# Splitting one PSUM eviction between ScalarE and VectorE, and taking a statistics sum ahead of the first product, in a fused normalise, shift and convolve kernel

## The chip, the cores and the metric

One Trainium2 chip, one core. The metric is the time of one execution on the device in microseconds (us). The measured times are medians of several executions; a profile is one execution taken by the hardware profiler.

## What is computed

The input x is 32 x 384 x 64 x 64 in f32 (batch, channel, row, column). Each group of 12 channels of an image is normalised over its 12 x 64 x 64 values. The normalised tensor is then moved, eight channels at a time, by one of 48 rounded offsets (pixels that come from outside are zero) and convolved with a 5x5 Gaussian whose centre carries the fraction of the offset. The input is added to the result:

```
x = x + _L0_conv_ref(_gn(x), L0_conv_offset)
disp = _displace(x.reshape(B, P, cpp, h, w), off_int).reshape(B, C, h, w)
sub = offset - lax.stop_gradient(off_round)
kernel = jnp.exp(-jnp.sum(d * d, axis=-1) / (2.0 * SIGMA ** 2))
out = lax.conv_general_dilated(disp, kw, ..., feature_group_count=C, ...)
```

Shift and Gaussian are separable, so that each is a product with a matrix along the rows and then one along the columns.

## The kernel before, in words

**Tiling.** A step handles 2 images x 24 channels (a superblock of channels). There are 16 superblocks and 16 steps in each: 256 steps, numbered t. The 24 channels lie as 4 lanes (32 partitions each) of 6 channels in 3 positions. A step's input fills one of 16 slots of `xin`; its result is added into the same slot, stored from there, and then the slot is loaded anew.

**Stages of a step.**
- VectorE takes statistics of each slot six steps ahead, in three pieces (`statistics`, line 440).
- GpSimd prepares `summands` (256, 258). For each pair of steps TensorE sums them over the partitions with a product against `ones` (`sum_stats`, 600), VectorE reduces that (`sums`, 447), and GpSimd makes scale and bias (`coefficients`, 273 to 284), two pairs ahead.
- ScalarE normalises one half of the slot (546) and GpSimd the other (293) into `norm`.
- TensorE forms the row product into `yp` (`y_product`, 608). `yp` has four PSUM banks, one for each lane, and one buffer only.
- ScalarE evicts all of `yp` to `y` in one instruction of 1536 columns (`copy_y`, 555). It signals `y_ready`.
- TensorE forms the column product into `xp` (`x_product`, 617), position 2 first, then 0 and 1.
- VectorE adds `xp` to the slot in two instructions: `add_x` part 0 (459, 512 columns), part 1 (462, 1024 columns). ScalarE issues the stores (571), SyncE the loads (194).

**Order on TensorE.** `two_steps` (639) covers a pair. With Y(t) for the row products of a step, X(t) for its column products and S for `sum_stats`, the order in the steady state is Y(t), X(t-1), S, Y(t+1), X(t), Y(t+2), X(t+1), S, and so on. So X always lies between two Y, and hides the eviction; between X(t-1) and Y(t+1) there is also an S, between X(t) and Y(t+2) there is none. I call a step with an S an even step and the one without an odd step. Waits ahead of a Y: `y_ready` (the eviction), `norm0_ready`, `norm1_ready`, `mats_ready`. S waits for `result0_ready`, that is for `add_x` part 0, since both use one PSUM bank.

**Order on VectorE.** A step (485) is: statistics 0 and 1 of the slot six ahead; in step 15 of a superblock `swap_rows` (424, three copies of new row matrices); `add_x` part 0 of t-1; statistics 2; `add_x` part 1; in step 0 `swap_columns` (430); in even steps `sums`; in step 9 `values` (414).

**Head.** Before the first product only the sum of pair 0 is taken. `sum_stats` for pair 1 comes after Y of the second step (662 to 664), and GpSimd's `coefficients(1)` (311) runs inside its step 0, after the normalisation of the second step. ScalarE's `normalise` of the third step needs those coefficients, and it stands ahead of `copy_y` of the second step in ScalarE's program.

All of this is an order written out by hand for each engine. The first and last superblocks are unrolled; the middle is a hardware loop.

Of the kernel before, what the change touches and what calls it, by code (L numbers as in the profile page):

```python
# [45 lines left out]
def displaced_conv(nc: bass.Bass, x: bass.AP, offset: bass.AP, out: bass.AP):  # L46
# [7 lines left out]
    with ExitStack() as ctx:  # L54
# [90 lines left out]
        norm1_free = sem("norm1_free")  # L145
        y_done = sem("y_done")
        y_ready = sem("y_ready")
        x_started = sem("x_started")
        x_done = sem("x_done")
        result0_ready = sem("result0_ready")  # L150
# [55 lines left out]
        def _(pool):  # L206
# [95 lines left out]
            normalise(0, 0, 0, first=True)  # L302
            column_matrices(0)
            make_summands(1, 1, early=True)

            def step(c, s, head, tail):
                t, p = STEPS * c + s, STEPS // PAIR * c + s // PAIR
                if not (tail and s == STEPS - 1):
                    normalise(t + 1, (s + 1) % STEPS, STEPS // PAIR * c + (s + 1) // PAIR, first=head and s == 0)
                if head and s == 0:  # L310
                    coefficients(1, 1, early=True, used=False)
                if not (tail and s // PAIR + LEAD >= STEPS // PAIR):
                    if s % PAIR == 0:
                        make_summands(p + LEAD, (s // PAIR + LEAD) % RING)
                    else:
                        coefficients(p + LEAD, (s // PAIR + LEAD) % 2)
                if not tail:
                    if s == 2:
                        whole_distances(c + 1)
                    if s == 4:  # L320
                        full_distances(c + 1)
                    if s == 10:
                        column_matrices(c + 1)
# [3 lines left out]
        def _(dve):  # L327
# [127 lines left out]
            def add_x(t, s, part):  # L455
# [4 lines left out]
                else:  # L460
                    at = xin[:, s, 0:4, :].rearrange("p (k h) f -> p h k f", h=QP)
                    nc.vector.tensor_tensor(at, xp[:, 0:2], at, ALU.add).then_inc(result1_ready, 1)  # L462

            def all_statistics(s):
                for part in range(CHUNKS):
                    statistics(0, s, part)
# [8 lines left out]
            all_gains()  # L475
            values(0)
            all_statistics(2)
            swap_columns(0)
            swap_rows(0)
            all_statistics(3)  # L480
            sums(1, 1, early=True)
            all_statistics(4)
            all_statistics(5)
# [1 line left out]
            def step(c, s, head, tail):  # L485
                t, p = STEPS * c + s, STEPS // PAIR * c + s // PAIR
                start = head and s == 0
                far = (s + AHEAD) % STEPS
                c_far = c + (s + AHEAD) // STEPS
                more = not (tail and s + AHEAD >= STEPS)  # L490
                s_old = (s - 1) % SLOTS
                ring_used = far % PAIR == 0 and not (head and s + AHEAD < PAIR * RING)
                if more:
                    statistics(c_far, far, 0, p + LEAD + 1 if ring_used else None)
                    statistics(c_far, far, 1)
                if s == STEPS - 1 and not tail:
                    swap_rows(c + 1)
                if not start:
                    add_x(t - 1, s_old, 0)
                if more:  # L500
                    statistics(c_far, far, 2)
                if not start:
                    add_x(t - 1, s_old, 1)
                if s == 0 and not head:
                    swap_columns(c)
                if s % PAIR == 0 and not (tail and s // PAIR + LEAD >= STEPS // PAIR):
                    sums(p + LEAD, (s // PAIR + LEAD) % 2, read=True)
                if not tail and s == 9:
                    values(c + 1)
# [5 lines left out]
        def _(act):  # L515
# [35 lines left out]
            def copy_y(t, v, first):  # L551
                act.wait_ge(y_done, t + 1)
                if not first:
                    act.wait_ge(x_done, ADDS * (t - 1))  # L554
                nc.scalar.activation(y[:, v].rearrange("p k r a m -> p a (k r) m"),  # L555
                                     yp[:, :, 0:POS * P].rearrange("p a (n m) -> p a n m", m=32),
                                     ACT.Copy).then_inc(y_ready, 1)

            square(0, 0)
# [35 lines left out]
        @block.tensor  # L595
        def _(pe):


            def sum_stats():
                nc.tensor.matmul(xp[:, 3, 1, 0:PAIR * GROUPS * 9], ones[:, :],  # L600
                                 summands[:].rearrange("p t n s -> p (t n s)"),
                                 start=True, stop=True).then_inc(stat_summed, 1)

            def y_product(k, v):
                for r in range(R):
                    for a in range(LANES):
                        rows = slice(32 * a, 32 * a + 32)
                        last = nc.tensor.matmul(yp[:, a, P * k:P * (k + 1)], norm[rows, v, r, P * k:P * (k + 1)],  # L608
                                                ay[rows, k, r, :], start=(r == 0), stop=(r == R - 1))
                if k == POS - 1:  # L610
                    last.then_inc(y_done, 1)

            def x_product(k, v):
                for r in range(R):
                    for h, m in ((0, 0), (1, 0), (0, 1), (1, 1)):
                        rows, outs = slice(64 * h, 64 * h + 64), slice(64 * m, 64 * m + 64)
                        last = nc.tensor.matmul(xp[outs, 2 * (k // 2) + h, k % 2, HW * r:HW * (r + 1)],  # L617
                                                y[rows, v, k, r].rearrange("p a m -> p (a m)")[:, outs], ax[rows, k],
                                                start=True, stop=True)
                if k > 0:  # L620
                    last.then_inc(x_done, 1)

            def x_products(v, results):

                pe.sem_inc(x_started, 1)
                x_product(2, v)
                pe.wait_ge(result1_ready, results)
                pe.sem_inc(x_started, 1)
                x_product(0, v)
                x_product(1, v)  # L630

            def begin_y(number, evicted):
                if evicted is not None:
                    pe.wait_ge(y_ready, evicted)
                pe.wait_ge(norm0_ready, number)
                pe.wait_ge(mats_ready[0], number)
                y_product(0, 0)

            def two_steps(one, head=False, more=True, last=False):

                two, three = one + 1, one + 2
                if not isinstance(one, int):
                    two, three = pe.snap(two), pe.snap(three)
                pe.wait_ge(norm1_ready, one)
                pe.wait_ge(mats_ready[1], one)
                y_product(1, 0)
                pe.wait_ge(mats_ready[2], one)
                y_product(2, 0)
                if not head:
                    pe.wait_ge(result0_ready, one)  # L650
                    x_products(1, one)
                    if more:
                        pe.wait_ge(summands_ready, one)
                        pe.wait_ge(result0_ready, two)
                        sum_stats()
                pe.wait_ge(y_ready, one)
                pe.wait_ge(norm0_ready, two)
                y_product(0, 1)
                pe.wait_ge(norm1_ready, two)
                y_product(1, 1)  # L660
                y_product(2, 1)
                if head:
                    pe.wait_ge(first_summands, LEAD)
                    sum_stats()
                    pe.wait_ge(first_sums, LEAD)
                    pe.wait_ge(summands_ready, one)
                    sum_stats()
                if more:
                    pe.wait_ge(sums_ready, one)
                pe.wait_ge(ax_ready, one)  # L670
                pe.wait_ge(result0_ready, two)
                x_products(0, two)
                if not last:
                    begin_y(three, two)

            pe.wait_ge(filled, FILLS)
            pe.wait_ge(first_summands, 1)
            sum_stats()
            begin_y(1, None)
            two_steps(1, head=True)  # L680
            with pe.Fori(PAIR + 1, PAIR * (PAIRS - LEAD) + 1, PAIR) as one:
                two_steps(one)
            for p in range(PAIRS - LEAD, PAIRS):
                two_steps(PAIR * p + 1, more=False, last=p == PAIRS - 1)
            pe.wait_ge(y_ready, TOTAL)
            pe.wait_ge(result0_ready, TOTAL + 1)
            x_products(1, TOTAL + 1)

# [20 lines left out]
```

## Time and profile before

| | |
|---|---|
| median of 3 runs | 1280.02 us (1278.77 to 1281.33) |
| profiled execution, its own time | 1280.09 us |
| its span, first to last instruction | 1278.3 us |
| mean granted TensorE clock | 0.994 |
| busy: TensorE matmul, VectorE, ScalarE, GpSimd | 94%, 77%, 55%, 51% |
| DMA | 403.06 MB, mean 315 GB/s |

Times in rows are us from the start of the span, durations in us or, where marked, ns. "PE" is TensorE's matmuls and "PEld" its weight loads, "DVE" VectorE, "ACT" ScalarE, "POOL" GpSimd. A name with q is the engine's queue. Profiled execution and median differ by 0.07 us.

### The profile page before, as it was taken

How to read it: one execution, taken by the hardware profiler on the slowest of the kernel's cores; microseconds unless marked ns; L12 is line 12 of the kernel's file. 1: busy time of each engine (PE TensorE's matmuls, PEld its weight loads, DVE VectorE, ACT ScalarE, POOL GpSimd, SP SyncE). 2: the span in 40 equal slices, each digit the busy share in tenths (PEclk: the TensorE clock that was granted, in tenths of full speed). 3: DMA queues.
4: the chain of work that ended last, by engine and by line, in shares of the span. 5: the costliest groups of instructions: out<-in, count | busy, mean ns of one | idle time of the engine just before them, and what ended most of it. 6: DMA issues, size and time to landing. Idle time of an engine off the chain costs nothing.

```text
span 1278.3 us, 110940 instructions
## 1 busy us (share of the span) xinstructions
PE 1200.4 (94%) x49408; PEld 1140.1 (89%) x49408; DVE 990.3 (77%) x1530; ACT 708.4 (55%) x595; POOL 658.1 (51%) x1478
## 2 busy tenths in 40 slices
PE   2899999999999999999999999999999999999995
PEld 2799999999999999999999999999999999999995
DVE  5788787778778778787778778778787788778862
ACT  3464655656555565655646555565555656555552
POOL 4645545554554645545554554645545554554540
PEclk9899999999999999999999999999999999999998
DMA  9699999999999999999999999999999999999854
GB/s 314 218 327 332 320 333 329 331 326 325 323 334 329 324 329 331 327 323 335 319 332 331 324 317 340 330 324 331 319 336 317 335 325 324 332 328 326 290 169 151
DMA packets 409768, 403.06 MB, mean 315 GB/s; under 512 B 16528, under 2 KB 409744, under 8 KB 409744
## 3 DMA queue, kind: packets, MB, share of 16 engines
q1 hardware_dynamic: 204944, 201.41, 48.9%
q10 hardware_dynamic: 204800, 201.36, 47.3%
q8 instruction: 12, 0.20, 0.1%
q14 instruction: 12, 0.10, 0.0%
HBM read 201.38 MB, written 201.33 MB: 315 GB/s over the span
## 4 chain that ended last, share of the span: by engine, by line
PE 81%; ACT 13%; issue 4%; DVE 1%; POOL 1%; ACTq 0%; POOLq 0%; DVEq 0%
PE yp L608 59%; PE xp L617 18%; ACT y L555 13%; PE xp L600 3%; DVE stats L440 0%; ACTq L554 0%; DVE xin L462 0%; POOL t_int L231 0%; POOL t_full L237 0%; POOL grid_i L211 0%; POOL var L280 0%; POOL rstd L282 0%; POOL norm L293 0%; DVE both L447 0%; DVE sub L378 0%
## 5 line engine op out<-in xcount | busy, mean ns | idle before, releaser
L608 PE MATMUL yp<-ay,norm 32*128 32x128 f32 x24576 | 762.3, 275 | 45.2 <-ACT y L555 35.3
L608 PEld LDWEIGHTS yp<-ay,norm 32*128 32x128 f32 x24576 | 716.9, 188 | 65.1 <-issue 50.7
L555 ACT ACTIVATE y<-yp 128x1536 f32<-128x1536 f32 x256 | 371.5, 1451 | 467.5 <-PE yp L608 467.5
L440 DVE BATCH_NORM_STATS2 stats<-xin 128x6 f32<-128x512 f32 x768 | 509.4, 692 | 0.1
L617 PE MATMUL xp<-ax,y 64*64 64x64 f32 x24576 | 420.8, 221 | 5.9 <-issue 4.6
L617 PEld LDWEIGHTS xp<-ax,y 64*64 64x64 f32 x24576 | 384.7, 135 | 37.4 <-issue 6.9
L459 DVE TENSOR_TENSOR xin<-xp,xin 128x512 f32<-128x512 f32 x256 | 176.9, 691 | 252.6 <-PE xp L617 251.1
L293 POOL TENSOR_SCALAR norm<-xin,rstd,bias 128x768 f32<-128x768 f32 x256 | 252.4, 986 | 201.3 <-PE yp L608 166.2
L462 DVE TENSOR_TENSOR xin<-xp,xin 128x1024 f32<-128x1024 f32 x256 | 309.2, 1208 | 7.1 <-PE xp L617 7.1
L546 ACT ACTIVATE norm<-xin,bias,rstd 128x768 f32<-128x768 f32 x256 | 261.7, 1023 | 58.5 <-issue 42.8
L273 POOL TENSOR_TENSOR mean_sq<-both 128x4 f32<-128x4 f32 x128 | 25.5, 199 | 269.4 <-DVE both L447 267.4
L282 POOL TENSOR_TENSOR rstd<-var,mhalf 128x4 f32<-128x4 f32 x128 | 132.4, 1035 | 10.0
L600 PE MATMUL xp<-summands,ones 128*128 128x36 f32 x256 | 53.1, 292 | 21.0 <-POOL summands L258 21.0
L600 PEld LDWEIGHTS xp<-summands,ones 128*128 128x128 f32 x256 | 38.5, 190 | 29.6 <-issue 21.0
L536 ACT ACTIVATE next_ay<-t_msk,same 128x768 f32<-128x768 f32 x32 | 32.5, 1020 | 9.4 <-issue 7.6
L256 POOL TENSOR_SCALAR summands<-stats 128x24 f32<-128x24 f32 x128 | 27.6, 216 | 19.0 <-DVE stats L440 8.0
L258 POOL TENSOR_TENSOR summands<-stats 128x12 f32<-128x12 f32 x128 | 27.3, 213 | 19.5 <-POOL summands L256 19.3
L231 POOL TENSOR_TENSOR t_int<-grid,place 128x960 f32<-128x960 f32 x16 | 28.7, 1795 | 7.0 <-DVEq L394 7.0
L284 POOL TENSOR_TENSOR bias<-minus_mean,rstd 128x4 f32<-128x4 f32 x128 | 26.7, 208 | 10.0
L280 POOL TENSOR_TENSOR var<-spread,mean_sq 128x4 f32<-128x4 f32 x128 | 26.3, 206 | 10.0
L278 POOL TENSOR_TENSOR spread<-inner,both 128x4 f32<-128x4 f32 x128 | 25.9, 203 | 10.7
L275 POOL TENSOR_SCALAR inner<-both 128x4 f32<-128x4 f32 x128 | 25.4, 199 | 10.1
(54 smaller groups left out, 191.0 us busy)
## 6 DMA issues: line engine op xcount, KB each, us to landing
xin<-in_x_dram SPq DMA_DIRECT2D x512, 384.0 KB, 5.3
out_dram<-xin ACTq DMA_DIRECT2D x512, 384.0 KB, 4.3
off<-in_L_conv_offset_dram SPq DMA_DIRECT2D x1, 48.0 KB, 3.2
```

The source lines that it names most:

```text
L231: pool.tensor_tensor(t_int[:], grid[:, None, :, :].to_broadcast([P, POS, KINDS, HW]), place[:, bass.ds(POS * c, POS), :].unsqueeze(3).to_b ...
L282: pool.tensor_tensor(rstd[:, v], var[:, v], mhalf[:, :], ALU.pow).then_inc(small, 1)
L293: pool.tensor_scalar(norm[:, s % 2, :, cols].rearrange("p r (q w) -> p q r w", w=HW), xin[:, s, QG:].rearrange("p q (r w) -> p q r w", w=H ...
L440: nc.vector.bn_stats(stats[:, s // PAIR % RING, s % PAIR, n, :], xin[:, s].rearrange("p (g q) f -> p q f g", g=GROUPS)[:, n]).then_inc(bn_ ...
L459: nc.vector.tensor_tensor(at, xp[:, 2:4, 0], at, ALU.add).then_inc(result0_ready, 1)
L462: nc.vector.tensor_tensor(at, xp[:, 0:2], at, ALU.add).then_inc(result1_ready, 1)
L536: nc.scalar.activation(next_ay[:].rearrange("p n r (m b) -> p n (r m) b", b=B)[:, :, :, part], t_msk[:, :, 0:R].rearrange("p n r m -> p n ...
L546: nc.scalar.activation(norm[:, s % 2, :, cols].rearrange("p r (q w) -> p q r w", w=HW), xin[:, s, 0:QG].rearrange("p q (r w) -> p q r w", ...
L555: nc.scalar.activation(y[:, v].rearrange("p k r a m -> p a (k r) m"), yp[:, :, 0:POS * P].rearrange("p a (n m) -> p a n m", m=32), ACT.Cop ...
L600: nc.tensor.matmul(xp[:, 3, 1, 0:PAIR * GROUPS * 9], ones[:, :], summands[:].rearrange("p t n s -> p (t n s)"), start=True, stop=True).the ...
L608: last = nc.tensor.matmul(yp[:, a, P * k:P * (k + 1)], norm[rows, v, r, P * k:P * (k + 1)], ay[rows, k, r, :], start=(r == 0), stop=(r == ...
L617: last = nc.tensor.matmul(xp[outs, 2 * (k // 2) + h, k % 2, HW * r:HW * (r + 1)], y[rows, v, k, r].rearrange("p a m -> p (a m)")[:, outs], ...
```

## The change

VectorE gets an instruction that evicts lane 3 of `yp` (384 columns), between its statistics and `swap_rows`/`add_x`; ScalarE's eviction covers lanes 0 to 2 (1152 columns). A new semaphore, `last_lane_ready`, is waited for beside `y_ready` in three places on TensorE. In the head the sum of pair 1 is taken ahead of the first product: VectorE's statistics of slot 3 stand ahead of the two swaps, and GpSimd's `coefficients(1)` ahead of its step 0.

```diff
@@ gpsimd
             make_summands(1, 1, early=True)
+            coefficients(1, 1, early=True, used=False)
@@ gpsimd, step
-                if head and s == 0:
-                    coefficients(1, 1, early=True, used=False)
@@ vector
+            def copy_last_lane(t, v):
+                dve.wait_ge(y_done, t + 1)
+                nc.vector.tensor_copy(y[:, v].rearrange("p k r a m -> p a (k r) m")[:, LANES - 1],
+                                      yp[:, LANES - 1, 0:POS * P].rearrange("p (n m) -> p n m", m=32)).then_inc(last_lane_ready, 1)
...
             all_statistics(2)
+            all_statistics(3)
             swap_columns(0)
             swap_rows(0)
-            all_statistics(3)
             sums(1, 1, early=True)
@@ vector, step
                     statistics(c_far, far, 1)
+                copy_last_lane(t, s % 2)
                 if s == STEPS - 1 and not tail:
                     swap_rows(c + 1)
@@ scalar, copy_y
-                nc.scalar.activation(y[:, v].rearrange("p k r a m -> p a (k r) m"),
-                                     yp[:, :, 0:POS * P].rearrange("p a (n m) -> p a n m", m=32),
+                nc.scalar.activation(y[:, v].rearrange("p k r a m -> p a (k r) m")[:, 0:LANES - 1],
+                                     yp[:, 0:LANES - 1, 0:POS * P].rearrange("p a (n m) -> p a n m", m=32),
@@ tensor, begin_y
                     pe.wait_ge(y_ready, evicted)
+                    pe.wait_ge(last_lane_ready, evicted)
@@ tensor, two_steps
                 pe.wait_ge(y_ready, one)
+                pe.wait_ge(last_lane_ready, one)
                 pe.wait_ge(norm0_ready, two)
...
                 if head:
-                    pe.wait_ge(first_summands, LEAD)
-                    sum_stats()
                     pe.wait_ge(first_sums, LEAD)
@@ tensor, start and end
             sum_stats()
+            pe.wait_ge(first_sums, 1)
+            pe.wait_ge(first_summands, 2)
+            sum_stats()
             begin_y(1, None)
...
             pe.wait_ge(y_ready, TOTAL)
+            pe.wait_ge(last_lane_ready, TOTAL)
```

## Rows read from the trace of the kernel before

**Rows 1.** The page: busy time of the engines; chain that ended last, by engine.
```profile
PE 1200.4 (94%) x49408; PEld 1140.1 (89%) x49408; DVE 990.3 (77%) x1530; ACT 708.4 (55%) x595; POOL 658.1 (51%) x1478
...
PE 81%; ACT 13%; issue 4%; DVE 1%; POOL 1%; ACTq 0%; POOLq 0%; DVEq 0%
```
**Rows 2.** Waits: who waited <- for whom: us in total, times, longest.
```profile
PE yp L608 <- ACT y L555: 35.3, 122, 1.6
```
**Rows 3.** Timeline of a pair of steps, all engines: start, duration, engine, line, operation.
```profile
603.79 0.69 DVE L459 TENSOR_TENSOR xin<-xp,xin 128x512 f32<-128x512 f32 x1 [1.19 <-PE xp L617]
...
604.58 0.30 PEld L600 LDWEIGHTS xp<-summands,ones 128*128 128x128 f32 x2
...
606.23 1.30 DVE L440 BATCH_NORM_STATS2 stats<-xin 128x6 f32<-128x512 f32 x2
...
607.81 1.49 PEld L617 LDWEIGHTS xp<-ax,y 64*64 64x64 f32 x96
...
608.03 1.45 ACT L555 ACTIVATE y<-yp 128x1536 f32<-128x1536 f32 x1 [1.17 <-PE yp L608]
...
608.58 0.69 DVE L459 TENSOR_TENSOR xin<-xp,xin 128x512 f32<-128x512 f32 x1 [1.04 <-PE xp L617]
...
609.70 1.49 PEld L608 LDWEIGHTS yp<-ay,norm 32*128 32x128 f32 x48 [0.39 <-issue]
```
**Rows 4.** Timeline of the tail: an X and a Y with the eviction long finished.
```profile
1247.51 0.43 PEld L617 LDWEIGHTS xp<-ax,y 64*64 64x64 f32 x21 [0.49 <-issue]
1248.01 2.77 PEld L608 LDWEIGHTS yp<-ay,norm 32*128 32x128 f32 x96
```
**Rows 5.** Groups by line and shape: count | busy, mean ns | idle before.
```profile
L555 ACT ACTIVATE y<-yp 128x1536 f32<-128x1536 f32 x256 | 371.5, 1451 | 467.5 <-PE yp L608 467.5
...
L462 DVE TENSOR_TENSOR xin<-xp,xin 128x1024 f32<-128x1024 f32 x256 | 309.2, 1208 | 7.1 <-PE xp L617 7.1
...
L459 DVE TENSOR_TENSOR xin<-xp,xin 128x512 f32<-128x512 f32 x256 | 176.9, 691 | 252.6 <-PE xp L617 251.1
...
L424 DVE COPY ay<-next_ay 128x512 f32<-128x512 f32 x48 | 17.6, 423 | 8.9 <-PE yp L608 8.1 <-issue 0.8
L525 ACT ACTIVATE t_isq<-t_int 128x960 f32<-128x960 f32 x16 | 16.1, 1005 | 6.4 <-issue 4.0 <-POOL t_int L231 2.4
```
**Rows 6.** TensorE's queue at line 636: the wait instruction, min/median/max ns.
```profile
L636 PEldq EVENT_SEMAPHORE  x128: 51/51/51, 23.3 to 1253.3; - x128
```
**Rows 7.** Timeline of VectorE around `values` (step 9) of one superblock.
```profile
621.61 1.30 DVE L440 BATCH_NORM_STATS2 stats<-xin 128x6 f32<-128x512 f32 x2
623.00 0.69 DVE L459 TENSOR_TENSOR xin<-xp,xin 128x512 f32<-128x512 f32 x1
```
**Rows 8.** Timeline of VectorE around `swap_rows` (step 15) of one superblock.
```profile
646.50 1.10 DVE L424 COPY ay<-next_ay 128x512 f32<-128x512 f32 x3 [0.58 <-PE yp L608]
...
651.80 0.69 DVE L459 TENSOR_TENSOR xin<-xp,xin 128x512 f32<-128x512 f32 x1 [0.66 <-PE xp L617]
```
**Rows 9.** Timeline of the head, all engines.
```profile
23.45 5.08 PE L608 MATMUL yp<-ay,norm 32*128 32x128 f32 x96 [6.67 <-DVE ay L424]
...
30.10 2.96 PE L608 MATMUL yp<-ay,norm 32*128 32x128 f32 x96 [1.57 <-ACT y L555]
...
33.44 0.20 DVE L447 TENSOR_REDUCE both<-xp 128x12 f32<-128x36 f32 x1 [7.64 <-PE xp L600]
...
36.33 1.03 ACT L546 ACTIVATE norm<-xin,bias,rstd 128x768 f32<-128x768 f32 x1 [6.28 <-POOL bias L284]
...
46.33 1.63 PE L617 MATMUL xp<-ax,y 64*64 64x64 f32 x96
```
**Rows 10.** Busy by stretch: us, PE, PEld, DVE, ACT, POOL busy (x), clock, DMA share, GB/s.
```profile
40.00:45.00 5.00, 5.00 (x134) 4.88 (x132) 4.11 (x6) 0.00 (x0) 4.61 (x8) 0.50 0.06 18
...
600.00:700.00 100.00, 96.98 (x4020) 92.27 (x4023) 79.91 (x121) 57.62 (x49) 51.96 (x118) 1.00 1.00 327
```
**Rows 11.** DMA issues by line: KB each, median us from issue to landing.
```profile
xin<-in_x_dram SPq DMA_DIRECT2D x512, 384.0 KB, 5.3
```

More of the change, by code:

```diff
@@ L147, in displaced_conv @@
         y_ready = sem("y_ready")
+        last_lane_ready = sem("last_lane_ready")
         x_started = sem("x_started")
```

## The prediction

> **What bounds the kernel now.** I read the page first. TensorE is busy 94% of the span, and the chain that ended last runs over it for 81% and over ScalarE for 13% [rows 1]. So TensorE sets the pace, and something on ScalarE holds it up at some places. The list of waits says which: 122 times, 35.3 us in total, a row product waited for the eviction [rows 2]. There are 128 pairs of steps, so that is once in a pair. The timeline of a pair shows where: in the odd step. The weight loads of X end at 607.81 + 1.49 = 609.30, the eviction at 608.03 + 1.45 = 609.48, and the first weights of the next Y go in at 609.70, 0.22 behind the eviction [rows 3]. In the tail, where ScalarE is long done, the same hand-over from X to Y takes 1248.01 - (1247.51 + 0.43) = 0.07 us [rows 4], against 0.40 here. An odd step can give back at most 0.33 us. In an even step S fills the time of the eviction, and what S waits for is another thing: `add_x` part 0 ends at 603.79 + 0.69 = 604.48 and S starts at 604.58 [rows 3]. So in an even step VectorE is on the path, with a slack near nothing behind `add_x`, and that is where the new instruction goes in.
>
> **The part that ScalarE gives up.** From 960 to 1536 columns ScalarE goes from 1005 to 1451 ns, 0.77 ns a column; the proportional share of the whole would be 0.94 [rows 5]. 384 columns fewer save 0.30 to 0.36 us; I take 0.31. The eviction then ends at 609.17, and with the 0.22 to the weights Y could start at 609.39, practically at the 609.37 that the bare hand-over allows. Against that stands one more wait in TensorE's queue; a wait there has 51 ns [rows 6]. Its cost lies between nothing (it is passed while the array still works on X) and some 0.15 (three such durations). I take 0.05. **Odd step: 0.31 - 0.05 = 0.26 us, 122 times: -31.7 us** (bounds 0.15 and 0.33, that is -18 and -40). In the even step the additional wait lies behind S and costs nothing, as long as S covers it; without the cover it would be the same 0.05.
>
> **The part that VectorE takes on.** The copy reads 384 columns from PSUM. Nothing in the trace is that. VectorE's adds that read PSUM go from 691 to 1208 ns between 512 and 1024 columns: 1.01 ns a column and 0.17 fixed, so 0.56 us. Its copy within SBUF does 512 columns in 423 ns [rows 5], which scaled to 384 is 0.32. I take 0.56, from the row nearest in its source. Consecutive instructions overlap: three of 0.423 fill 1.10 [rows 8], so 0.08 each, and the copy keeps VectorE for 0.48.
>
> The page "VectorE: DVE Perf Modes" of the Trainium skill, section "Mode 2×_2P — use both read ports for one tensor", says that an f32 copy doubles its rate only with source and destination in SBUF, because PSUM has a single read port. By it the price is the upper one, 0.56; no row here shows such a copy from PSUM. Going by the SBUF row instead, the late steps below would cost 5 us instead of 15.8, and the forecast would come out 11 us lower.
>
> In an ordinary step VectorE's two statistics end at 606.23 + 1.30 = 607.53, half a microsecond before the row product is seen done at 608.03. From there to `add_x` part 0 at 608.58 it idles on, and the even step's `add_x` at 603.79 has the same wait ahead of it, 1.19 against 1.04 [rows 3]. That is 0.55 of room for 0.48: the copy costs nothing, but with 0.07 to spare and less if VectorE wakes late (a swap that waited for the same signal began 0.07 later in its step, at 646.50). Its result is there at 608.6, long before ScalarE's. With the odd steps 0.26 shorter the statistics before the even step's copy still end some 0.25 ahead.
>
> The cover fails where VectorE has more to do. **`values`, step 9:** the following statistics end at 621.61 + 1.30 = 622.91, and `add_x` of step 10 starts at 623.00 [rows 7], with no idle time at all. After the change the copy starts at 622.83, `add_x` at 623.31, while TensorE, 0.26 ahead, would have it at 622.74: 0.57 late. Step 10 is even, S waits for just that, and so does everything behind it. **`swap_rows`, step 15:** the copy stands ahead of it and pushes it by 0.48; `add_x` of the next step, an even one again, had 0.66 idle ahead of 651.80 [rows 8]. Two copies (0.96) against 0.66 + 0.08 of overlap and the 0.26 that TensorE is early: late by 0.96 - 0.74 + 0.26 = 0.48. Each comes 15 times: **15 x (0.57 + 0.48) = +15.8 us.** The new matrices themselves come 0.48 later, at about 647.3 for the first, ahead of the Y that uses them.
>
> GpSimd and the loads do not enter. GpSimd is busy 51% [rows 1]. Loads and stores run at 327 GB/s and would need at most 327 x 9.60 / 9.34 = 336 (9.60 us is a pair of steps, from 600.1 to 609.7); a load lands 5.3 us after issue [rows 11], and statistics touch a slot about six steps, 28 us, after that. A total gain of 23 us is smaller than this store of time, even if transfers could not go faster at all [rows 10].
>
> **The head.** Now: Y(0) at 23.45, Y(1) at 30.10; only then S of pair 1, the reduction at 33.44, coefficients until 36.33, when ScalarE can normalise the third step, and only behind that evict Y(1). The third Y cannot start before that eviction, and X(1) starts at 46.33 [rows 9]. At 40 to 45 the granted clock is 0.50, the lower level of 1.2 GHz, after TensorE had been left without products from 30.10 + 2.96 = 33.06 until that normalisation and that eviction were through [rows 9, 10]. After: S of pair 1 waits for slot 3's statistics and delays Y(0) to about 24.1; the chain reduction to coefficients, 36.33 - 33.44 = 2.9, starts at 24.3 and is over at 27.2, below Y(0), which takes 5.08 as now and ends at 29.1. Evictions until 30.3, Y(1) to 33.3, S of pair 2 to 33.7, reduction, X(0) from 34.0 to 35.6. VectorE, which waits for that reduction, does two statistics and then its lane until 35.7, so the third Y starts at 35.9 (that is the new wait in the head) and, with the clock kept up, X(1) at 38.8. **46.33 - 38.8 = -7.5 us**; if the clock still fell for one Y and one X, they would take twice as long at most, 2.96 + 1.63 = 4.6 less; if GpSimd's late normalisation got in the way, up to 4 less.
>
> **Sum.** -31.7 + 15.8 - 7.5 = -23.4. From the profiled 1280.09 that gives 1256.7; the median of the runs is 1280.02, the same within 0.1.
>
> **The rivals.**
> (A) The lateness after `values` and `swap_rows` does not reach TensorE, because VectorE has unseen reserves. For it: 77% busy. Against: 623.00 follows 622.91 directly. Then -39.2: 1240.9.
> (B) The wait is only exchanged: TensorE's queue needs as long for the added waits in the odd step as ScalarE saves. Then the 31.7 are gone, the late steps cost 0.26 less each (+8), the head stays: 1280.6, no change. Against: a wait is 51 ns, not 300.
> (C) The copy is slower than its room in every even step. One place, one price: `add_x` part 0 and with it S are late by what the copy keeps VectorE beyond 0.55. The point from which the kernel gets slower than before by over 0.2% is 26 us / 128 = 0.20, that is 0.75 of occupancy or a copy of 0.83 us. At 0.95 us: 98 x 0.32 + 30 x 0.39 = +43, 1300. For it: source rows of 32 in strides, two engines reading `yp` at once. Against: ScalarE's eviction and VectorE's `add_x` already overlap in PSUM, and `add_x` has its usual 0.69 there [rows 3].
> The section "Specifications" of the same page of the Trainium skill places ScalarE closer to PSUM and VectorE closer to SBUF, which speaks for (C); the fixed 0.17 of the add rows is what the trace shows of it.
> (D) The head gives nothing, or gives back what it gains: 1264.
>
> **How the numbers follow.** The forecast 0.62; (A) 0.12; (B) 0.06; (C) 0.08; (D) 0.12. The forecast's own bounds: with 0.33 an odd step and a copy of 0.32, -40 + 7 - 7.5, 1239.6; with 0.15 and a poorer head, -18 + 13 - 4, 1271. The range 1240 to 1271 takes in (D) and (A). A measurement tells about 0.2% from nothing, 2.6 us. Faster by more: forecast, (A), (D) 0.86; same: (B) 0.06; slower: (C) 0.08.
>
> **What would show it.** In the profile after: PE's wait for ScalarE nearly gone in the steady state; ScalarE's eviction at 1.14 us; a VectorE copy of 0.56 between the statistics and `add_x`; a pair of steps at 9.34 instead of 9.60 us; twice in a superblock S some 0.5 late, for VectorE; no stretch at clock 0.50 around 40 us; X(1) at 39. I am wrong if the copy lasts over 0.63, if S waits for `add_x` in ordinary even steps, or if the odd hand-over stays above 0.2 us.

## The result, and the profile after

The changed kernel takes 1251.1 us (median of 4 runs, 1250.54 to 1251.46) against 1280.55 for the kernel before in the same session: a ratio of 0.9772, 95% interval 0.9755 to 0.9788. It is 2.3% faster. The forecast was 1256.7, range 1240 to 1271. The profiled execution has a span of 1249.7 against 1278.3.

The page after, against [rows 1, 5]:

```profile
PE 1197.8 (96%) x49408; PEld 1140.0 (91%) x49408; DVE 1125.7 (90%) x1786; ACT 626.6 (50%) x595; POOL 658.6 (53%) x1478
...
PE 82%; DVE 11%; issue 5%; POOL 1%; DVEq 0%; ACT 0%; POOLq 0%
...
L561 ACT ACTIVATE y<-yp 128x1152 f32<-128x1152 f32 x256 | 289.6, 1131 | 446.4 <-PE yp L614 446.4
...
L466 DVE COPY y<-yp 128x384 f32<-128x384 f32 x256 | 142.1, 555 | 84.4 <-PE yp L614 84.4
L459 DVE TENSOR_TENSOR xin<-xp,xin 128x512 f32<-128x512 f32 x256 | 176.4, 689 | 17.6 <-PE xp L623 2.7
```

ScalarE's 13% of the chain are gone, and VectorE stands there with 11%. The eviction fell from 1451 to 1131 ns; the lane costs VectorE 555 ns. VectorE's idle time before `add_x` part 0 fell from 252.6 us to 17.6: the copy fills that gap.

TensorE's waits after, against [rows 2] (who waited <- for whom: us, times, longest):

```profile
PE xp L606 <- DVE xin L459: 10.9, 30, 0.5
...
PE yp L614 <- issue: 4.1, 2, 2.7
PE yp L614 <- ACT y L561: 1.2, 1, 1.2
```

122 waits for ScalarE became one, in the head. New are exactly 30, S behind `add_x` part 0.

The timeline of an odd step after, against [rows 3]:

```profile
603.97 1.49 PEld L623 LDWEIGHTS xp<-ax,y 64*64 64x64 f32 x96
...
604.11 0.56 DVE L466 COPY y<-yp 128x384 f32<-128x384 f32 x1 [0.43 <-PE yp L614]
604.19 1.13 ACT L561 ACTIVATE y<-yp 128x1152 f32<-128x1152 f32 x1 [2.01 <-PE yp L614]
...
604.73 0.69 DVE L459 TENSOR_TENSOR xin<-xp,xin 128x512 f32<-128x512 f32 x1
...
605.53 2.80 PEld L614 LDWEIGHTS yp<-ay,norm 32*128 32x128 f32 x96
```

The last weights of X end at 603.97 + 1.49 = 605.46, those of Y start at 605.53: 0.07 us, the bare hand-over of [rows 4], where it had been 0.40. ScalarE ends at 605.32; its 0.21 to the next weights lead to the same 605.53, so both limits now coincide. VectorE sees the row product 0.08 earlier than ScalarE and starts `add_x` as early in X as before (0.76 behind its first weights).

From one Y to the next, averaged over the 14 middle superblocks (starts of the first weights in the trace), an odd step fell from 4.777 to 4.449 us. Ordinary even steps stayed at 4.82. Step 10 rose from 4.823 to 5.373 and step 0 from 4.829 to 5.147. A superblock fell from 76.81 to 75.04 us.

Step 9 to 10 of one superblock, against [rows 7]:

```profile
608.14 1.31 DVE L440 BATCH_NORM_STATS2 stats<-xin 128x6 f32<-128x512 f32 x2
...
609.37 0.54 DVE L466 COPY y<-yp 128x384 f32<-128x384 f32 x1
609.83 0.68 DVE L459 TENSOR_TENSOR xin<-xp,xin 128x512 f32<-128x512 f32 x1
...
610.56 0.30 PEld L606 LDWEIGHTS xp<-summands,ones 128*128 128x128 f32 x2 [0.62 <-DVE xin L459]
```

Statistics, copy and `add_x` follow one another without a gap, and S stands behind them.

TensorE in the head, against [rows 9, 10]:

```profile
31.73 2.96 PE L614 MATMUL yp<-ay,norm 32*128 32x128 f32 x96 [1.25 <-ACT y L561]
...
37.14 1.79 PE L614 MATMUL yp<-ay,norm 32*128 32x128 f32 x50
41.60 2.94 PE L614 MATMUL yp<-ay,norm 32*128 32x128 f32 x46 [2.67 <-issue]
```

```profile
40.00:45.00 5.00, 3.40 (x66) 3.17 (x69) 0.99 (x2) 0.41 (x1) 1.51 (x2) 0.63 0.05 16
45.00:50.00 5.00, 5.00 (x162) 4.81 (x158) 3.99 (x7) 1.75 (x2) 1.70 (x6) 0.69 0.49 160
```

The third row product starts at 37.1 instead of 42.1, but breaks off after 50 of its 96 records and stands for 2.67 us, waiting for nothing that the profile shows. The granted clock falls behind it again (0.63, a mixture of 2.4 and 1.2 GHz; a window from 41.4 to 48.0 has 0.50). Of the 5 us that the third row product starts earlier, 1.0 is left at the fifth (52.4 against 53.4).

### The profile page after: what moved, and what is told of

It reads as the page before. It is cut to its first block, busy times and chain, and to the rows that moved or that the text cites. A ratio compares the mean times of both kernels' runs of the same rounds, so it can differ in the third digit from the quotient of the medians.

```text
span 1249.7 us, 111549 instructions
## 1 busy us (share of the span) xinstructions
PE 1197.8 (96%) x49408; PEld 1140.0 (91%) x49408; DVE 1125.7 (90%) x1786; ACT 626.6 (50%) x595; POOL 658.6 (53%) x1478
## 4 chain that ended last, share of the span: by engine, by line
PE 82%; DVE 11%; issue 5%; POOL 1%; DVEq 0%; ACT 0%; POOLq 0%
PE yp L614 53%; PE xp L623 25%; PE xp L606 4%; DVE stats L440 3%; DVE xin L462 2%; DVE xin L459 2%; DVE t_msk L414 1%; DVE ay L424 1%; DVE y L466 1%; POOL t_int L232 0%; POOL t_full L238 0%; DVEq L183 0%; POOL grid_i L212 0%; DVEq L465 0%; POOL summands L257 0%
## 5 line engine op out<-in xcount | busy, mean ns | idle before, releaser
L561 ACT ACTIVATE y<-yp 128x1152 f32<-128x1152 f32 x256 | 289.6, 1131 | 446.4 <-PE yp L614 446.4
L294 POOL TENSOR_SCALAR norm<-xin,rstd,bias 128x768 f32<-128x768 f32 x256 | 252.6, 987 | 163.2 <-PE yp L614 127.4
L466 DVE COPY y<-yp 128x384 f32<-128x384 f32 x256 | 142.1, 555 | 84.4 <-PE yp L614 84.4
L459 DVE TENSOR_TENSOR xin<-xp,xin 128x512 f32<-128x512 f32 x256 | 176.4, 689 | 17.6 <-PE xp L623 2.7
L259 POOL TENSOR_TENSOR summands<-stats 128x12 f32<-128x12 f32 x128 | 27.3, 213 | 19.5 <-POOL summands L257 19.3
```

The lines of the kernel that those rows point to most:

```text
L294: pool.tensor_scalar(norm[:, s % 2, :, cols].rearrange("p r (q w) -> p q r w", w=HW), xin[:, s, QG:].rearrange("p q (r w) -> p q r w", w=H ...
L459: nc.vector.tensor_tensor(at, xp[:, 2:4, 0], at, ALU.add).then_inc(result0_ready, 1)
L466: nc.vector.tensor_copy(y[:, v].rearrange("p k r a m -> p a (k r) m")[:, LANES - 1], yp[:, LANES - 1, 0:POS * P].rearrange("p (n m) -> p n ...
```

## The experiments

All times are medians; ratios are to the kernel before on the same chip, with 95% intervals. Step times come from the traces as above.

**Can the two parts be had alone?** By the order of the programs, the split in every step with the old head cannot run (this is read from the code, not tried): VectorE's `sums(1)` waits there for a sum that TensorE takes after Y(1), Y(1) would wait for lane 3 of Y(0), and its copy stands behind `sums(1)`. The new head is what makes the full split possible.

**head_only.** The kernel before with the reordered head.

```diff
+            coefficients(1, 1, early=True, used=False)   # gpsimd, ahead of step 0
...
+            all_statistics(3)                            # vector, ahead of the swaps
...
+            pe.wait_ge(first_sums, 1)                    # tensor, ahead of begin_y(1, None)
+            pe.wait_ge(first_summands, 2)
+            sum_stats()
```

> The kernel before with the head's reordering alone, no split of the eviction. Prediction as put down: 7.5 us less, 1273. What the trace of the changed kernel suggests: there the fifth row product starts only 1.0 us earlier than before (52.4 against 53.4), because TensorE stops for 2.7 us for nothing the profile shows as a wait ('issue') while it runs the third row product, at 38.9. If that is a property of the head and not of the split, this kernel shows the same stop and is worth 1 to 2 us: 1278.5 to 1279.5. If the head is worth its 7.5 and the split hid it, 1273.

Measured: 1278.21 us, ratio 0.9986 (0.9977 to 0.9995), so 1.8 us less (by the interval 0.6 to 2.9), which excludes 7.5. The timeline shows the same stop in the same product:

```profile
37.04 1.82 PE L607 MATMUL yp<-ay,norm 32*128 32x128 f32 x51
42.21 2.22 PE L607 MATMUL yp<-ay,norm 32*128 32x128 f32 x45 [3.35 <-issue]
```

The waits for ScalarE's eviction are all still there (36.3 us, 124 times). The head is worth 0.6 to 2.9 us by itself; the rest of the change is the split.

**odd_only.** The changed kernel, with the lane on VectorE in odd steps only.

```diff
-                copy_last_lane(t, s % 2)
+                if s % 2 == 1:
+                    copy_last_lane(t, s % 2)
...
+                lanes = LANES - v
+                nc.scalar.activation(y[:, v].rearrange("p k r a m -> p a (k r) m")[:, 0:lanes],
...
                 pe.wait_ge(y_ready, one)
-                pe.wait_ge(last_lane_ready, one)
```

(Each copy now stands for two steps, so that it raises `last_lane_ready` by 2.)

> The changed kernel, but VectorE takes its lane in odd steps only; in even steps ScalarE evicts all four. Theory: in an even step the statistics sum S covers the full eviction, so ScalarE's 0.32 us more cost nothing, while VectorE is rid of the copy exactly where add_x part 0 came late (step 10 by 0.55 us, step 0 of a superblock by 0.33). Then 15 x (0.55 + 0.33) = 13 us are saved but for some 1.5: 1251.1 - 11.7 = 1239.4. Rival: the late steps come from the work of values and swap_rows alone, and the copy only stands beside them: no change, 1251. Second rival: S does not cover a full eviction once the pairs are shorter, and even steps grow by up to 0.3: 1251 - 12 + 38 = 1277.

Measured: 1240.34 us, 0.9688 (0.9675 to 0.9701), faster than the change by 11. Steps 10 and 0 fell to 4.910 and 4.848, ordinary even steps stayed at 4.82, odd ones at 4.449. TensorE's 30 waits for `add_x` shrank to one:

```profile
PE xp L608 <- DVE xin L459: 0.2, 1, 0.2
```

Both rivals are refuted. The late steps came from the copy on top of `values` and `swap_rows`, and S does cover a full eviction.

**odd_old_head.** The same with the head of the kernel before; GpSimd's and VectorE's parts of the head, which the cut below leaves out, are the old ones too.

```diff
-            sum_stats()                                  # tensor, ahead of begin_y(1, None)
...
+                    pe.wait_ge(first_summands, LEAD)     # tensor, head, behind y_product(2, 1)
+                    sum_stats()
```

> As odd_only, with the head of the kernel before (statistics sum of pair 1 behind the second row product). It gives the worth of the head in the presence of the split. By the trace 1 to 2 us slower than odd_only: about 1241. By the prediction 7.5 slower: 1247.

Measured: 1241.51 us, 0.9698 (0.9685 to 0.9712). The medians differ by 1.2 us and the intervals overlap: 1 to 2 us fits, 7 does not.

**values_8.** The changed kernel with `values` one step earlier.

```diff
-                if not tail and s == 9:
+                if not tail and s == 8:
                     values(c + 1)
```

> The changed kernel with values(c+1) in VectorE's step 8 instead of 9, so that the copy that it delays is that of step 9, an odd step, behind whose add_x part 0 no S waits. Theory: step 10 falls from 5.37 to 4.82 us, 15 times: -8.2 us, 1243. If it is VectorE's total work that costs there and not the place, the delay only moves: 1251. Should step 9 itself grow because the lane comes late for the odd hand-over, 1243 plus up to 15 x 0.4 = 1249.

Measured: 1242.88 us, 0.971 (0.9697 to 0.9724): 8.2 less. Step 10 fell from 5.373 to 4.823; step 9, which now carries the delay, is 4.467 against 4.448. The same work costs VectorE the same and TensorE 0.02 instead of 0.55, since no S stands behind an odd `add_x`. (In the profiled execution the head is shorter too, 42.91 to X(1) against 44.47, though its code is the same; the part on the head below says why.) What is left are the 15 waits from `swap_rows`:

```profile
PE xp L606 <- DVE xin L459: 3.7, 15, 0.3
```

**three_waits.** What a wait in TensorE's queue costs.

```diff
                     pe.wait_ge(last_lane_ready, evicted)
+                    pe.wait_ge(stat_summed, 1)
+                    pe.wait_ge(first_summands, 1)
+                    pe.wait_ge(first_sums, 1)
```

> The changed kernel with three more waits behind last_lane_ready ahead of the first row product of each odd hand-over, on semaphores that were satisfied in the head. By the prediction's term, 0.05 us for an added wait: 3 x 0.05 x 125 = +19 us, 1270. By the trace of the changed kernel the wait at line 641 is passed at 605.17 while X still runs until 605.33, and costs nothing; three more of 51 ns then end at 605.37, about when ScalarE's eviction is seen: 0 to +4 us, 1251 to 1255.

Measured: 1255.36 us, 0.9803 (0.9787 to 0.9819). Six of the eight odd steps of a superblock grew by 0.035 to 0.038 us and two (5 and 13) by some 0.065; the two late steps shrank by 0.036 each, and a superblock grew by 0.28. That is 4 us in all, far from 19. The queue of the changed kernel passes 125 waits for the lane in 51 ns each, the longest included (min/median/max):

```profile
L641 PEldq EVENT_SEMAPHORE  x125: 51/51/51, 52.0 to 1214.6; - x125
```

The one that the trace shows at 605.17 is over by 605.22, a tenth of a microsecond before X's last weights have begun. It costs nothing. In three_waits the trace has two instructions in its place, not four, since each of them carries two semaphores:

```profile
L643 PEldq EVENT_SEMAPHORE  x125: 51/51/51, 52.2 to 1219.2; - x125
L644 PEldq EVENT_SEMAPHORE  x127: 51/51/51, 36.7 to 1230.2; - x127
```

So the run prices one more instruction, not three: the two start 0.116 us apart, and the instruction behind them, which waits for ScalarE's eviction, starts 1.42 us behind X's first weights instead of 1.39. A second instruction just outlasts the lead of the queue. The expectation had counted three.

**copy_twice.** The price of rival (C).

```diff
                 dve.wait_ge(y_done, t + 1)
+                nc.vector.tensor_copy(spare[:].rearrange("p n a m -> p a n m")[:, LANES - 1],
+                                      yp[:, LANES - 1, 0:POS * P].rearrange("p (n m) -> p n m", m=32)).then_inc(spared, 1)
```

> The changed kernel, but VectorE copies the lane a second time, into a spare tensor, ahead of the real copy. It prices rival (C). Room theory: copy and add_x stand with 0.55 to 0.62 us of room for 0.46 of occupancy; a second copy makes add_x part 0 0.30 late in every even step and S, which has 0.06 of slack, 0.24 late: 96 x 0.24 = +23; step 10 and step 0 grow by 0.46 and 0.92: +21. 1295. If VectorE's lateness does not reach TensorE (rival A), no change, 1251. If VectorE simply becomes the bound by its total work, 1125.7 + 142 busy of the span: about 1280.

Measured: 1300.48 us, 1.0152 (1.0135 to 1.0169), 1.5% slower than before (1295 was expected). TensorE's wait, and the copies and `add_x` of an ordinary even step:

```profile
PE xp L610 <- DVE xin L461: 52.8, 124, 1.3
```

```profile
602.42 0.54 DVE L468 COPY spare<-yp 128x384 f32<-128x384 f32 x1
602.88 0.54 DVE L470 COPY y<-yp 128x384 f32<-128x384 f32 x1
603.34 0.68 DVE L461 TENSOR_TENSOR xin<-xp,xin 128x512 f32<-128x512 f32 x1
```

A copy keeps VectorE for 0.46. Ordinary even steps grew by 0.25 (5.07), step 10 by 0.77 (0.46 was expected) and step 0 by 0.89, odd steps by nothing, but for step 15 with 0.05. In an odd step the additional 0.46 is free; in an even one it costs 0.25, so 0.21 of room was left, of which `add_x` had 0.15 (it starts 1.07 behind X's first weights instead of 0.76) and S some 0.06.

**pad100 and pad200.** 100 or 200 increments of an otherwise unused semaphore at the start of TensorE's program.

```diff
+            for _ in range(100):
+                pe.sem_inc(padded, 1)
             pe.wait_ge(filled, FILLS)
```

> The changed kernel with 100 semaphore increments at the start of TensorE's program, where TensorE idles for 24 us anyway. Theory: the stop of 2.7 us at 38.9 is TensorE waiting for the next 16 KB block of its own instructions (a DMA of 16384 bytes on the instruction queue starts at 39.1 and work resumes at 41.6). Then the stop moves 100 instructions earlier in the stream, out of the third row product into X(0) or Y(1), and the time changes by 0 to -3 us, or +1 to +3 if the blocks fall worse in the tail. Rival: the stop is a hidden wait for data and stays in the third row product after about 50 matmul records; time unchanged.

> The same with 200 increments: the stop moves 200 instructions earlier, into Y(1) of the head or near its start, where TensorE waits for the eviction of Y(0) anyway. Theory: there it is partly hidden, and the head is 1 to 3 us shorter than in the changed kernel; tail unknown, plus or minus 2. Rival: unchanged place and time.

Measured: 1249.92 us (0.9762, 0.9746 to 0.9778) and 1262.89 us (0.986, 0.9843 to 0.9876). In pad100 the stop moved, from 50 records into the third row product to 2 records. Between the two places TensorE's program has 48 matmul records, as many weight loads, and 3 instructions of the queue: 99 instructions, the length of the padding within one. A wait for data would not move. In pad200 the increments themselves took 31 us, which the expectation had not counted, so that everything came 15 us later, and there the stop is gone:

```profile
40.45 4.87 PE L615 MATMUL yp<-ay,norm 32*128 32x128 f32 x96
46.58 2.96 PE L615 MATMUL yp<-ay,norm 32*128 32x128 f32 x96 [1.26 <-ACT y L562]
...
51.99 3.24 PE L615 MATMUL yp<-ay,norm 32*128 32x128 f32 x96
55.16 1.63 PE L624 MATMUL xp<-ax,y 64*64 64x64 f32 x96
```

From Y(0) to X(1) it takes 55.16 - 40.45 = 14.7 us, against 44.47 - 24.97 = 19.5 in the changed kernel. The prediction had 38.8 - 24.1 = 14.7. Its chain was right, but for the stop and what the clock does behind it.

**odd_v8.** odd_only and values_8 together.

> odd_only with values in step 8. What was late in odd_only is step 10 by 0.09 us and step 0 by 0.03. With the move step 10 falls to an ordinary 4.82: -1.3 us, 1239.0. If the two remedies did not overlap, 1240.3 - 8.2 = 1232.

Measured: 1238.34 us, 0.9676 (0.9663 to 0.9689). The two remedies overlap as expected: the interval touches that of odd_only, but in the trace step 10 fell from 4.910 to 4.819, and a superblock takes 74.22 us instead of 74.29.

**odd_v8_pad200w and odd_v8_pad100.** The paddings on odd_v8, the first with 200 waits on `filled` in place of increments.

> odd_v8 with 200 waits on a satisfied semaphore at TensorE's start in place of the 200 increments of pad200, which themselves took 31 us and delayed everything by 15 us. At 51 ns each they take 10 us and end ahead of the first sum. Theory of the instruction blocks: from Y(0) on the head is 4 to 5 us shorter, as in pad200, in which the stop in the third row product is gone; tail within 2 us. 1235 to 1237. If repeated waits are dropped when the program is built, or if the blocks fall worse in the tail, 1239 to 1241.

> odd_v8 with the 100 increments of pad100. In the changed kernel they brought 1.2 us; theory: the same here, 1238. If pad100 was noise, 1239.

Measured: 1238.64 us (0.9679, 0.9665 to 0.9692) and 1236.90 us (0.9676, 0.966 to 0.9691). Neither can be told from odd_v8. The 200 waits delay the start by only 1.2 us, and the stop is there again (2.48 us, 2 records into the third row product). This expectation, a head 4 to 5 us shorter, missed. The trace says why the stop stands where it does in pad100: the 200 waits became 100 instructions with two semaphores each. 99 of them have the padding's line, and the last one has the line of the `filled` wait behind it.

```profile
L684 PEldq EVENT_SEMAPHORE  x99: 51/51/51, 6.6 to 17.1; - x99
```

So this run was a second pad100 and did not repeat pad200's shift by 200 instructions. Whether pad200 lost its stop by the other place or by the later time can't be told from it; late_loads below bears on that. odd_v8_pad100 shows that the stops come at a regular distance:

```profile
39.10 2.95 PE L617 MATMUL yp<-ay,norm 32*128 32x128 f32 x94 [1.24 <-issue]
...
43.00 1.16 PE L626 MATMUL xp<-ax,y 64*64 64x64 f32 x64 [0.32 <-issue]
...
47.53 1.38 PE L617 MATMUL yp<-ay,norm 32*128 32x128 f32 x36 [1.05 <-issue]
...
51.70 0.34 PE L626 MATMUL xp<-ax,y 64*64 64x64 f32 x5 [1.24 <-issue]
```

From one stop to the next it is 126, 126 and 127 matmul records. With the weight loads and the queue's instructions between them that is about 256 instructions each time, and at each stop lies one DMA record of 16384 bytes (36.5, 40.5, 45.3 and 49.2).

**late_loads.** odd_v8, with the first loads held back.

```diff
             for s in range(SLOTS):
+                if s == 10:
+                    sync.wait_ge(y_done, 3)
                 load(0, s)
```

> odd_v8 with the first loads of slots 10 to 15 held back until the third row product is done. In the runs so far the stop in the third row product (2.4 to 2.7 us, shorter in the padded ones) came while, or just after, the 16 slots were loading at 350 GB/s until about 36 us; in pad200, where everything on TensorE came 15 us later, it was gone, and from Y(0) to X(1) took 14.7 us against 18.0 in odd_v8. Theory: TensorE's instruction block queues behind the loads. Then the stop is gone, X(1) starts at about 39.7 instead of 42.9, and the time is 3 to 5 us less than odd_v8: 1234.5. Rival: the block is asked for too late whatever the loads do; the stop stays, 1238.3.

Measured: 1239.52 us, 0.9686 (0.9673 to 0.9699): no gain, where 1234.5 was expected. The timeline of TensorE, and the stretches (the last two numbers are DMA share and GB/s):

```profile
36.23 1.79 PE L618 MATMUL yp<-ay,norm 32*128 32x128 f32 x50
38.47 1.61 PE L618 MATMUL yp<-ay,norm 32*128 32x128 f32 x46 [0.45 <-issue]
40.02 1.43 PE L627 MATMUL xp<-ax,y 64*64 64x64 f32 x81
...
46.08 0.45 PE L627 MATMUL xp<-ax,y 64*64 64x64 f32 x13
49.28 1.50 PE L627 MATMUL xp<-ax,y 64*64 64x64 f32 x83 [2.75 <-issue]
```

```profile
30.00:35.00 5.00, 3.71 (x124) 3.50 (x128) 1.49 (x5) 2.83 (x4) 1.09 (x4) 1.00 0.01 2
...
45.00:50.00 5.00, 2.25 (x106) 1.99 (x102) 1.20 (x3) 2.16 (x2) 2.62 (x6) 1.00 1.08 374
```

With the DMA engines idle the stop at record 50 shrank from 2.41 us (odd_v8) to 0.45, and X(1) starts at 40.0 instead of 42.9, 15.0 behind Y(0) at 25.00. Then the six late slots load at 374 GB/s, and a later stop, at the same place as one of 0.56 us in values_8, grows to 2.75. The place of a stop follows the count of instructions, its length the loads. The gain in time was lost to the second stop. In every one of these traces a DMA record of 16384 bytes on the instruction queue lies beside it (39.1 in the changed kernel, 36.0 and 47.0 here).

## Why the prediction was right

**The bound and the odd step.** Right in mechanism, the term too small. The step "0.31 - 0.05 = 0.26" measured 0.328: 0.32 came from ScalarE (0.31 assumed), and the 0.05 for an additional wait was nothing, as the hand-over shows, which is now the bare 0.07 of [rows 4]. The whole of the 0.33 to be had was taken. 122 times 0.328 is -40.0 against -31.7. A pair of ordinary steps takes 9.27 us (9.34 predicted).

**The copy.** 0.555 us against 0.56, occupancy 0.46 against 0.48. By "VectorE: DVE Perf Modes" of the Trainium skill, section "Why PSUM operands drop a tier", an f32 copy out of PSUM runs at the single rate; the 555 ns agree, with some 1.0 ns a column behind the fixed part of the adds. The section "Specifications" of the same page of the Trainium skill, by which ScalarE sits closer to PSUM, spoke for rival (C); this trace shows no additional price. The cover in ordinary steps held. One reading of the prediction was wrong here: "in an even step VectorE is on the path, with a slack near nothing behind `add_x`". What set S was TensorE itself. S starts 0.07 us behind the end of X's weights in ordinary even steps, before (604.58 against 603.02 + 1.49) and after, the bare hand-over of [rows 4], and `add_x` had some 0.06 us of slack.

**The late steps.** Right, in both places and on the engine named: 30 waits. Step 10 measured 0.55 (0.57 predicted), step 0 measured 0.32 (0.48): +13.0 against +15.8. odd_only and values_8 show the cause.

**The head.** The step that failed: "**46.33 - 38.8 = -7.5 us**". head_only gives -1.8. Each event of the chain came in the order described, and pad200 takes exactly the 14.7 us from Y(0) to X(1). In the changed kernel X(1) starts at 44.47, 5.7 later than predicted, and the trace shows three pieces of that, together 4.9. Y(0) starts at 24.97 instead of 24.1: GpSimd's first `summands` instruction for pair 1 took 1.02 us where it usually takes 0.22. TensorE then stands for 2.67 us for its own instructions. Behind that stop the clock falls. In values_8, whose head is the same, it did not:

```profile
41.36 1.61 PE L614 MATMUL yp<-ay,norm 32*128 32x128 f32 x46 [2.67 <-issue]
...
40.00:45.00 5.00, 3.18 (x139) 2.97 (x141) 2.19 (x4) 1.52 (x2) 2.02 (x2) 1.00 0.16 55
```

From the end of the stop to X(1) it takes 42.91 - 41.36 = 1.55 us there and 44.47 - 41.60 = 2.87 in the changed kernel, so that the clock costs 1.3 up to X(1). The same stop was followed by a fall in some traces (head_only, odd_only) and not in others (values_8, odd_v8). I had priced in only the clock and GpSimd's late normalisation, and had called a stretch at 0.50 around 40 us a thing that would be gone.

**The sum.** -40.0 + 13.0 - 1.8 = -28.8, and the spans differ by 28.6. Two errors of opposite sign, -8.3 on the odd step and +5.7 on the head, and 2.8 less on the late steps, left the forecast some 5 us high. That it came so near is partly luck. Rival (A) is refuted by the 30 waits, (B) by the odd hand-over of 0.07 us, (D) is partly true: the head gives a quarter of what was forecast. Rival (C) did not come true, but copy_twice gives its law: at twice the copy the kernel is 1.5% slower than before.

Loads and stores went to 334 GB/s between 600 and 700 us without a wait on VectorE's statistics, as assumed.

## What to carry to other kernels

When an engine evicts under the cover of another product, look at each kind of step by itself: here only every second eviction was exposed, and moving a quarter of that one alone brought 3.1 to 3.2%, while moving it in all steps brought 2.3%. Before giving work to an engine with idle time on average, look for the steps in which it has none and ask who waits behind it there; shifting a rare task by one step was worth 8 us. A wait that is satisfied early cost nothing here as long as the queue ran ahead of the engine. When instructions are added to a program as a test, count them in the trace: waits written one by one came out as half as many instructions.

## What was not expected of the hardware

TensorE can stop for its own instructions where it runs through them for the first time. With the new head and without padding the stop took 2.4 to 3.5 us near 40 us, while a block of 16 KB is fetched; it took 0.45 us where the DMA engines were idle. The text on the kernel before calls the first and last superblocks unrolled. On TensorE only the first pair of steps and the last two are; its loop begins 32 records into the third row product, so that the stops from record 50 on lie in the first pass of the loop, and later passes show none. The last two pairs have them again, in both kernels: six stops in a row, each 126 or 127 records behind the one before, together 6.1 us in the changed kernel and 6.5 in the one before, for instance

```profile
1228.66 2.05 PE L614 MATMUL yp<-ay,norm 32*128 32x128 f32 x58 [1.39 <-issue]
...
1242.24 1.55 PE L623 MATMUL xp<-ax,y 64*64 64x64 f32 x62 [1.86 <-issue]
```

In the kernel before, the block's record lies at 40.7, and TensorE comes to the place of the stop only at 44.6, when the block has long landed; no stop shows there. The new head comes to the same place at 38.9 and finds the block missing. Whether pad200 is free of the stop because its block boundary lies in X(0), because its loads are long done, or both, stays open, and so does which instruction asks for the block.

200 semaphore increments took 31 us on TensorE's queue, about 0.15 each. The 100 instructions that wait for two semaphores took 0.106 each from 6.6 us on, where TensorE had nothing to do until 16 us in any case.
